# A two-layer graph attention kernel: x1 turned one block later, low parts awaited within a product, reciprocals made a tile ahead

## What is computed

```python
x = _layernorm(x + _L0_gnn_ref(x, src, dst, ...), axis=-1)      # x1
x = _layernorm(x + _L1_gnn_ref(x, edge_index, ...), axis=-1)
...
out = relu((agg + res).reshape(n, H * DOUT))      # L0: 12 heads, agg = sum of alpha * ft
...
h = gat_conv(x, edge_index, W1, a_src1, a_dst1, b1, HEADS, HID, True)   # x @ W1: 768 x 1024
h = relu(layer_norm(h, g1, be1)) + (h0 @ Wr1 + br1)                     # x @ Wr1: 768 x 1024
```

## Time and profile before

| | us |
|---|---|
| three runs | 1126.82, 1128.27, 1129.32 |
| median | 1128.27 |
| span of the profiled execution | 1124.5 |
| TensorE busy | 1052.4 (94%) |
| VectorE busy | 950.9 (85%) |
| ScalarE busy | 642.3 (57%) |
| GpSimd busy | 142.6 (13%) |

### The profile page before, as it was taken

How to read it: one execution, slowest core, us unless ns; L and a number is a source line. 1 busy time by engine, 2 the same in 40 slices (tenths; PEclk the granted TensorE clock), 3 DMA queues, 4 the chain that set the end, 5 groups by cost and what they waited for, 6 DMA issues and landing times.

```text
span 1124.5 us, 20563 instructions
## 1 busy us (share of the span) xinstructions
PE 1052.4 (94%) x8048; PEld 906.7 (81%) x8048; DVE 950.9 (85%) x1530; ACT 642.3 (57%) x938; POOL 142.6 (13%) x155
## 2 busy tenths in 40 slices
PE   6986999898989899999999999999999999999995
PEld 4665666666666667999999999999988888888884
DVE  7989999999999999976853999999987873488874
ACT  8658999999999997223111567666612212233331
POOL 1000000000000000000072112020400153411111
PEclk9998999999999999999999999999999999999998
DMA  4061020202020305533237310204042134443211
GB/s 149 1 237 42 3 92 1 93 1 92 1 92 1 98 1 197 174 107 110 84 116 268 109 47 2 84 1 151 20 169 59 41 99 170 141 174 113 75 63 44
DMA packets 39911, 98.99 MB, mean 88 GB/s; under 512 B 4492, under 2 KB 17184, under 8 KB 39814
## 3 DMA queue, kind: packets, MB, share of 16 engines
q1 hardware_dynamic: 39814, 97.66, 25.4%
HBM read 70.74 MB, written 26.90 MB: 87 GB/s over the span
## 4 chain that ended last, share of the span: by engine, by line
PE 62%; DVE 20%; ACT 9%; issue 8%; DVEq 0%; POOL 0%; POOLq 0%; ACTq 0%
PE psum L1097 14%; PE psum L1006 14%; PE psum L1058 12%; DVE R L1662 9%; PE psum L1126 9%; DVE R L1648 5%; ACT R L1265 4%; PE psum L1021 4%; ACT R L1281 3%; PE psum L753 2%; PE psum L1074 1%; PE psum L938 1%; DVE LC L1634 1%; PE psum L1109 1%; PE psum L889 1%
## 5 line engine op out<-in xcount | busy, mean ns | idle before, releaser
L938 PE MATMUL psum<-ident,R 128*128 128x128 f32 (+3 forms) x1200 | 156.8, 279 | 38.4 <-ACT R L1265 37.8
L938 PEld LDWEIGHTS psum<-ident,R 128*128 128x128 f32 (+3 forms) x1200 | 127.6, 142 | 79.0 <-ACT R L1265 66.5
L1662 DVE CUSTOM_DVE_ANT_0 R<-R,LC 128x1250 f32<-128x1250 f32 x120 | 176.0, 1470 | 0.2 <-DVE LC L1634 0.2
L1265 ACT ACTIVATE R<-R,row_max 128x1250 f32<-128x1250 f32 x120 | 161.6, 1346 | 2.0 <-DVE row_max L1662 1.6
L952 PE MATMUL psum<-R 128*64 128x256 f32 (+3 forms) x1200 | 147.1, 383 | 0.6 <-ACT R L1281 0.6
L1281 ACT COPY R<-psum 128x1280 f32<-128x1280 f32 x120 | 143.5, 1196 | 1.5 <-PE psum L938 1.5
L1006 PE MATMUL psum<-w_hi,x1T_hi 128*128 128x256 f32 (+1 forms) x480 | 136.1, 284 | 1.2 <-DVE x1T_lo L1745 0.8
L1006 PE MATMUL psum<-w_hi,x1T_lo 128*128 128x256 f32 (+1 forms) x480 | 134.7, 281 | 0.0
L1006 PE MATMUL psum<-w_lo,x1T_hi 128*128 128x256 f32 (+1 forms) x480 | 134.3, 282 | 0.0
L1648 DVE SCALAR_TENSOR_TENSOR R<-R 128x1250 f32<-128x1250 f32 x80 | 122.5, 1533 | 0.0
L2131 POOL TENSOR_TENSOR rstd<-rstd,minus_half 128x1 f32<-128x1 f32 (+1 forms) x40 | 33.8, 845 | 664.1 <-DVE rstd L1675 664.1
(11 more groups left out here) (225 smaller groups left out, 2475.2 us busy)
## 6 DMA issues: line engine op xcount, KB each, us to landing
R<-rows_spill SPq DMA_DIRECT2D x20, 625.0 KB, 5.2
rowbuf<-rows_spill SPq DMA_DIRECT2D x14, 625.0 KB, 5.1
lc_spill<-LC SPq DMA_DIRECT2D x9, 625.0 KB
LC<-lc_spill SPq DMA_DIRECT2D x9, 625.0 KB, 5.4
res_spill<-colbuf SPq DMA_DIRECT2D x36, 128.0 KB, 2.8
R<-res_spill SPq DMA_DIRECT2D x9, 512.0 KB, 3.5
R<-in_x_dram SPq DMA_DIRECT2D x1, 3456.0 KB
res_spill<-R SPq DMA_DIRECT2D x9, 384.0 KB
```

Of the source, the lines that this page charges most:

```text
L938: last = e.transpose(turn0[r % 2][0:m, s, 0:n_dst], ring[0:n_dst, r % RING0, s * P:s * P + m], ident[0:n_dst, 0:n_dst])
L1265: e.activation(ring[0:m, r % RING0, :], ring[0:m, r % RING0, :], ACT.Exp, bias=row_max[0:m, r % RING:r % RING + 1], scale=-1.0, accum_out= ...
L1662: e.tensor_tensor_reduce(slot, slot, LC[0:m, i, :], -1.0, MIN_CEILING, ALU.add, ALU.min, row_max[0:m, r % RING:r % RING + 1]).then_inc(S.l ...
```

## The change

Four edits, all in this stage.

- `turn_after1`: tiles 2 to 7 are turned behind (1, i - 1) and no longer behind (2, i - 1). Tile 1 stays behind (1, 0), tile 8 behind (2, 7), tile 9 behind (0, 7).
- `gemm1`: a step waits for `x1T_hi` at its start. For block 2 and tiles 0 to 7 (`x_late`) the matmuls go part by part: 6 high x high, 6 with the low part of the weight, 6 with the low part of x1, and each part's wait stands ahead of it. For tile 0 and blocks 1 and 0 (`w_late`) those with the low part of the weight come last and are awaited there. Other steps have all waits at their start, as before.
- `first_recip(i)` is split off from `first_scaled(i)` and stands between the statistics and the normalisation of the tile before.
- `rest_x1(i - 1)` stands behind `first_scaled(i)` for every i from 2 on. Before, only tile 1's stood there; tile 2's stood behind `first_added(3)`, the others' behind `first_stats(i)`.

```diff
-        turn_after1 = {(2, i): i + 1 for i in range(1, NT - 2)}
-        turn_after1[(1, 0)] = 1
+        turn_after1 = {(1, i): i + 1 for i in range(NT - 3)}
+        turn_after1[(2, NT - 3)] = NT - 2
         turn_after1[(0, NT - 3)] = NT - 1
...
-                e.wait_ge(S.x1T_lo, i + 1)
+                e.wait_ge(S.x1T_hi, i + 1)
...
-                if b == WBUFS1 and i == 0:
+                x_late = b == 2 and i < NT - 2
+                w_late = b == WBUFS1 and i == 0 or i == 0 and b < 2
+                if w_late:
                     steps = [(k, part) for k in range(KT) for part in parts[0:2]] + [(k, parts[2]) for k in range(KT)]
+                elif x_late:
+                    steps = [(k, parts[0]) for k in range(KT)] + [(k, parts[2]) for k in range(KT)]
+                    steps += [(k, parts[1]) for k in range(KT)]
                 else:
                     steps = [(k, part) for k in range(KT) for part in (parts[0], parts[2], parts[1])]
                 for n, (k, (xs, ws)) in enumerate(steps):
-                    if n == (2 * KT if b == WBUFS1 and i == 0 else 0):
+                    if n == (2 * KT if w_late else KT if x_late else 0):
                         e.wait_ge(S.w1_lo, split_order1.index(b) + 1)
+                    if n == (2 * KT if x_late else 0):
+                        e.wait_ge(S.x1T_lo, i + 1)
...
+            def first_recip(i):
+                m = rows[i]
+                r = recip0[0:m, i % 2, :]
+                e.wait_ge(S.exp0, 4 * (U * (G0 - 1) + i // 2 + 1))
+                if i >= 2:
+                    e.wait_ge(S.normed0, i - 1)
+                e.tensor_scalar(r, den0[0:m, i, :], 1e-16, None, ALU.max).then_inc(S.recip0, 1)
+                e.wait_ge(S.recip0, 2 * i + 1)
+                e.reciprocal(r, r).then_inc(S.recip0, 1)
...
             for i in range(2, NT):
                 first_scaled(i)
-                if i == 2:
-                    rest_x1(1)
+                rest_x1(i - 1)
                 first_added(i)
-                if i == 3:
-                    rest_x1(i - 1)
                 first_stats(i)
-                if i >= 4:
-                    rest_x1(i - 1)
+                if i + 1 < NT:
+                    first_recip(i + 1)
                 first_norm(i)
```

More of the change, by code:

```diff
@@ L1684, in first_scaled @@
                 e.wait_ge(S.agg_kept, U * (G0 - 1) + i // 2 + 1)
-                e.tensor_scalar(r, den0[0:m, i, :], 1e-16, None, ALU.max).then_inc(S.recip0, 1)
-                e.wait_ge(S.recip0, 2 * i + 1)
-                e.reciprocal(r, r).then_inc(S.recip0, 1)
                 e.wait_ge(S.recip0, 2 * i + 2)
@@ L1823, in h_stats @@
                 norm_stats(NT + i, i, [xl1[0:rows[i], i, k, :] for k in range(H1)])
+            first_recip(0)
             first_scaled(0)
@@ L1827, in dve_program @@
             first_stats(0)
+            first_recip(1)
             first_scaled(1)
@@ L1834, in dve_program @@
             rest_w1(1)
+            first_recip(2)
             first_norm(1)
```

## The result

The changed kernel takes 1137.47 us (median of five, 1137.08 to 1138.83), the kernel before 1128.27: 9.2 us more, ratio 1.0088 with an interval of 1.0078 to 1.0099. It was forecast slower, 1136.0, in a range of 1131 to 1139. The profiled execution has a span of 1135.3 us (1124.5 before). The spans differ by 10.8 us and the medians by 9.2: a run's time stands 1.8 us above its own span (1137.08 over 1135.3), so of the 3.8 us that were read between median and span before, 2.0 were only that the profiled execution was one of the faster ones.

What follows compares the result with a forecast made beforehand. TensorE bound the stage at 6.95 us per x1 tile; the change would make VectorE's 8.00 us period rule. Last turn +7.35 plus a 0.4 us wait, together +7.7: span 1132.2, plus 3.8 to the median, 1136.0; range 1131 to 1139.

Steps and rivals of the forecast that it cites:

- The store in the loop: VectorE at tiles 2 to 8: the low part waits 1.57 us for its tile's store; period 8.00 us, not 6.30; chance 0.62.
- N: The start of a tile's normalisation on VectorE; N(2) is tile 2's, forecast to go from 454.59 to 454.13 us.
- Which of the two waits ends last: At the low part: store landing (N + 3.04) outlasts ScalarE's high part (N + 2.42); rival, high part rules: 1131.3, chance 0.06.
- The reciprocals: Made a tile ahead on VectorE, free in its 0.66 us wait for GpSimd; tile 2's normalisation 0.46 us earlier.
- Turn 2: TensorE's transposes of x1 tile 2: wait of 1.1 us instead of 2.29, start 0.46 us earlier.
- Turn 8: TensorE's transposes of x1 tile 8, two products behind the turn before: idle 3.1 us ahead, probably dropping the clock.
- (0, 9): TensorE's product one behind the last turn: new wait for tile 9's low part, taken as 0.4 us.
- Turn 9: TensorE's last x1 transposes, the yardstick for the span: start at 510.86 us against 503.51, +7.35; 1.4 us wait ahead.
- The split and the later turns: TensorE's low parts awaited within a product and turns one block later: cost nothing, gain nothing while VectorE's period rules.
- the case with a drop behind turn 9: TensorE's clock falls after its last x1 transposes, adding 1.7 us to 7.35: +9.1, 1137.4; chance 0.20.

## Why the prediction was right

- **The store in the loop**: right, and the main thing. Forecast: low part at N + 3.04, stall 1.57, period 8.00. Measured over the seven periods from tile 2 to 9: (512.68 - 455.55) / 7 = 8.16. Five of the seven are 8.06 to 8.11, the other two 8.30 and 8.43. The term was 0.16 us too small a tile, 1.1 us in all. I took 2.33 us for the landing from one row; in the changed kernel the landings are 2.3 to 3.0. And the upper bound of 2.5 was not read off ten stores, as the prediction says: a trace records the landings of six of the ten, and in the one before none had been waited for.
- **Which of the two waits ends last**: right. Taking the store away uncovered the other at 2.48 and 0.94 us against 2.42 and 0.95 worked out.
- **The reciprocals**: right that they are free; the wait for GpSimd ahead of the normalisation shrank from 0.66 to 0.30 us. Wrong that tile 2 gains 0.46: N(2) comes 8.79 us behind N(1) (455.55 - 446.76), not 8.10, and before it was 8.56. Tile 1's low part, which the change does not move, is reached earlier and then waits 0.61 us for its own store, whose landing took 3.0. I had put that wait at nothing, from the one landing of 2.3 in the trace of before. In the kernel without the store N(2) does come 8.09 behind N(1).
- **Turn 2** waits 1.05 us, forecast 1.1, and that is luck. Counted from N(1), the tile was forecast ready for its turn at 8.83 and came at 9.53; TensorE was forecast there at 7.7 and came at 8.5, since turn 1 did not wait for its tile but started 1.32 us behind N(1), not 0.73. Two errors of 0.7 to 0.8 us cancel.
- **Turn 8** waits 3.01, forecast 3.1.
- **(0, 9)** waits 0.75, forecast 0.4: the low part of tile 9 began 3.46 us behind its normalisation, not 3.04. In the eight other traces where it waited for the single store it was 3.43 to 3.75.
- **Turn 9**: I gave 1.4 us of waiting behind one drop of the clock; it is 0.25, because the clock stayed at 1.2 GHz for 6.8 us and not for the 3.4 that the earlier trace rows show. It still cost nothing here, as the prediction said it would not: TensorE arrived just ahead of the tile. A slower store, or a longer drop, would have told.
- **The split and the later turns are worth nothing while VectorE's period rules**: right, and alone they are worth nothing either.
- **The size**: +7.7 forecast, +9.2 measured. Between N(1) and turn 9 the forecast has 8.10 + 56.0 + 0.73 = 64.8 us and the trace 66.7: 1.1 of the 1.8 are the period, 0.7 the wait of tile 1. With 0.35 more at (0, 9) the three short terms would have made it +9.9. The trace has 9.2 to turn 9 and 0.9 behind it, 10.1 in all; the medians differ by 9.2, and the 0.9 us between the two is within the spread of single executions. So the mechanism is right, and a part of the nearness of 1136.0 to 1137.47 is luck. The 9.1 that I had given to the case with a drop behind turn 9 is nearly the same number by another way, and not what happened.

The Trainium skill, "DMA: Bandwidth & Descriptors" (anatomy of one DMA), has 2.9 us for this size by an estimate from its fit, which is stated for GpSimd's path. For SyncE's queue the traces here have less: 42 of the 78 recorded landings of x1 stores took 2.3 us.

## What to carry to other kernels

An in-order queue turns a wait into a loop as soon as an instruction that waits for its own tile's round trip (a store, another engine's copy) stands ahead of the next tile's work: write down the loop's period, and compare it with the engine that is to stay busy. An instruction that fills a wait is best placed by when its inputs are there, not by when its output is wanted; here six rows later were worth 11.7 us. Work out the first tile as well as the steady state: its wait was the term left out here. And an edit that shortens one wait by a microsecond or two can be judged only with the place where the last tile comes out, since that is all the rest of the kernel sees.

## What the runs showed of the hardware

- **Stores that land late.** In the thirteen traces with stores, 78 landings of x1 stores are recorded, six of ten in each. 42 took 2.29 to 2.33 us; in one of these a packet of the instruction queue (16 KB, 0.9 to 2.0 us) overlapped, at its very end. Of the 23 from there to 3.25 us, 10 had such a packet beside them. 13 took longer, and 12 of those had one in flight between their issue and their landing; the four slowest, 4.25 to 4.8 us, had it 1.0 to 2.3 us behind the issue. That is a coincidence seen often, not a cause shown: which of the sixteen DMA engines and whose instructions it was I did not try to separate, and one store (tile 1's, with the low parts moved alone) took 3.5 us without any.
- **Tile 1's store is seldom a fast one.** It landed in 2.30 us before, and in 2.4 to 4.1 in the twelve other traces (4.1 as the second of two stores). One trace was not enough to put its wait at nothing.
- **The clock after an idle time.** It was down at 0.50 (1.2 GHz) fourteen times in this stage over all the traces, eleven times for 3.4 us and three times for 6.8 (the changed kernel at turn 8, low parts moved alone at turn 9, store doubled at turn 8). The idle times ahead of the three were 3.01, 2.95 and 3.74 us; but 3.26, 3.38, 3.58 and 3.69 us were followed by 3.4 us only, as were the seven of 2.29 to 2.85. The idle time ahead does not tell which of the two it will be.
